# VectorE's order in the last layer's slots: the residue of the MLP tile ahead of the product for the heads

## The reference, cut to what matters

```python
# _L3_cond_ref: a dense MLP and the two best of 8 expert MLPs, hidden width 1024 each
g = einsum('bsh,hi->bsi', x, gate_w); u = einsum('bsh,hi->bsi', x, up_w)
cond = sum over (shared, top1, top2) of  w * einsum('bsi,ih->bsh', gelu(g) * u, down_w)
# _L3_ffn_ref
h = rmsnorm(cond, gamma1)
q = h @ Wq + bq                          # 16 heads of 16
k, v = split((h @ Wdown + bdown) @ Wup + bup)
att = softmax(einsum('bthd,btgd->bthg', q, k) / 4)   # per token, head against head
x1 = cond + (einsum('bthg,btgd->bthd', att, v) @ Wo + bo)
gate = softmax(rmsnorm(x1, gamma2) @ Wg + bg)
out = x1 + einsum('btd,edf,bte->btf', rmsnorm(x1, gamma2), We, gate)     # 8 experts
```

## Time and profile before

| | |
|---|---|
| median of 3 runs | 1732.6 us (1729.36 to 1734.81) |
| profiled execution, own time | 1735.44 us |
| its span | 1733.7 us |
| PE busy (matmul) | 1502.1 us, 87% |
| DVE busy | 1148.6 us, 66% |
| POOL busy | 652.6 us, 38% |
| ACT busy | 560.7 us, 32% |
| mean granted clock of PE | 0.917 of full |

### The profile page before, as it was taken

One profiled execution on the slowest core, in us unless ns is written; L12 is line 12 of the kernel. 1 busy time (PEld: TensorE's weight loads), 2 busy tenths in 40 slices (PEclk: granted clock), 3 DMA queues, 4 the chain that ended last, 5 costly groups with the idle time before them and its releaser, 6 DMA issues.

```text
span 1733.7 us, 19836 instructions
## 1 busy us (share of the span) xinstructions
PE 1502.1 (87%) x7420; PEld 1271.0 (73%) x7420; DVE 1148.6 (66%) x1977; ACT 560.7 (32%) x786; POOL 652.6 (38%) x268
## 2 busy tenths in 40 slices
PE   5997899999889978999998898987899889976628
PEld 4896799997668967899976676766677667755416
DVE  7597655546875976544568523378748975896984
ACT  2202243442232022344323343533452345332001
POOL 3320133322322201333222344366656654754552
PEclk9897989998998979899989899999999999996758
DMA  5300011111112100111111132221221212100001
GB/s 178 111 25 13 25 37 50 49 38 37 37 55 67 36 1 25 49 42 46 37 37 45 55 115 76 89 70 58 74 79 53 93 55 80 67 25 25 25 16 45
DMA packets 22592, 92.72 MB, mean 53 GB/s; under 512 B 3408, under 2 KB 3808, under 8 KB 22368
## 3 DMA queue, kind: packets, MB, share of 16 engines
q1 hardware_dynamic: 21168, 88.18, 15.4%
q10 hardware_dynamic: 1328, 3.27, 0.5%
HBM read 89.35 MB, written 2.10 MB: 53 GB/s over the span
## 4 chain that ended last, share of the span: by engine, by line
PE 34%; DVE 17%; POOL 7%; issue 7%; ACT 4%; DVEq 0%; POOLq 0%; ACTq 0%
PE bank L291 11%; PE bank L295 10%; PE bank L294 10%; POOL w_lo L413 4%; DVE G L313 3%; ACT w_hi L1030 2%; DVE bank L1532 2%; POOL VW L313 2%; DVE acc L1556 2%; DVE F L1556 1%; PE bank L759 1%; DVE acc L1688 1%; DVE hid_hi L1485 1%; PE bank L558 0%; PE bank L574 0%
## 5 line engine op out<-in xcount | busy, mean ns | idle before, releaser
L413 POOL TENSOR_TENSOR w_lo<-raw,w_hi 128x1536 fp32r<-128x1536 f32 x48 | 169.3, 3526 | 291.3 <-ACT w_hi L1030 265.6
L291 PE MATMUL bank<-x_hi,w_hi 128*128 128x512 f32 x448 | 188.3, 420 | 63.0 <-POOL w_lo L413 38.3
L401 POOL CAST w_hi<-raw 128x1024 fp32r<-128x1024 f32 (+2 forms) x42 | 49.8, 1185 | 481.4 <-issue 447.1
L1409 DVE TENSOR_TENSOR hid_lo<-F,hid_hi 128x1024 fp32r<-128x1024 f32 x64 | 82.3, 1288 | 166.6 <-ACT hid_hi L980 166.4
L294 PE MATMUL bank<-x_lo,w_hi 128*128 128x512 f32 x448 | 182.2, 407 | 0.0
L295 PE MATMUL bank<-x_hi,w_lo 128*128 128x512 f32 x448 | 181.6, 405 | 0.0
L291 PEld LDWEIGHTS bank<-x_hi,w_hi 128*128 128x128 f32 x448 | 89.2, 199 | 93.8 <-POOL w_lo L413 48.8
L404 POOL TENSOR_TENSOR w_lo<-raw,w_hi 128x1024 fp32r<-128x1024 f32 (+2 forms) x51 | 129.2, 2534 | 65.6 <-ACT w_hi L903 62.2
L975 ACT ACTIVATE F<-bank,vecs 128x512 f32<-128x512 f32 x128 | 81.2, 686 | 199.3 <-PE bank L295 199.3
L291 PE MATMUL bank<-hid_hi,w_hi 128*128 128x512 f32 x320 | 127.9, 400 | 11.4 <-DVE hid_lo L1487 6.5
L294 PE MATMUL bank<-hid_lo,w_hi 128*128 128x512 f32 x320 | 126.1, 394 | 0.0
(11 more groups left out here) (331 smaller groups left out, 4072.0 us busy)
## 6 DMA issues: line engine op xcount, KB each, us to landing
raw<-in_skill SPq DMA_DIRECT2D x32, 768.0 KB, 4.2
raw<-in_l SPq DMA_DIRECT2D x40, 512.0 KB, 3.5
raw<-in_shared SPq DMA_DIRECT2D x16, 768.0 KB, 4.2
K<-in_l3e SPq DMA_DIRECT2D x16, 512.0 KB, 3.6
raw<-in_l0c SPq DMA_DIRECT2D x12, 512.0 KB, 3.6
raw<-in_qkv SPq DMA_DIRECT2D x8, 768.0 KB, 4.2
xT<-in_x ACTq DMA_DIRECT2D x4, 512.0 KB, 7.1
VW<-in_l1w SPq DMA_DIRECT2D x1, 2048.0 KB, 8.9
```

Source lines behind the costliest of these rows:

```text
L291: i = nc.tensor.matmul(out, sh, mh, start=first, stop=False)
L413: nc.gpsimd.tensor_tensor(w_lo[n % W3_SLOTS][:], raw[n % 2][:], w_hi[n % W3_SLOTS][:].bitcast(F32), ALU.subtract).then_inc(w_ready.sem, 1)
L1409: v.tensor_tensor(hid_lo[u][:, hs, :], F[u][:], hid_hi[u][:, hs, :].bitcast(F32), ALU.subtract).then_inc(e1_hid.sem, 1)
```

## The change

In `hidden_lo`'s place: VectorE's queue gets the residue of the hidden tile right behind the gated product (and behind the special steps of that slot), and the product of the attention behind it. Nothing else moves, on VectorE or elsewhere.

```diff
                         finish3_first(p, i, x, y)
                     if 0 <= q < BATCH:
                         attention3_first(q, i, x, y)
+                    if b < BATCH:
+                        hidden_lo(TILES3 * b + i)
                     for h in range(16):
                         if HALF_SLOT[h] == i and 0 <= q < BATCH:
                             product(q, h)
                         if HALF_SLOT[h] == i + TILES3 and 0 <= p < BATCH:
                             product(p, h)
-                    if b < BATCH:
-                        hidden_lo(TILES3 * b + i)
```

## The result

The changed kernel takes 1753.2 us (median of 4 runs, 1749.96 to 1757.23) where the kernel before takes 1733.7 (4 runs). The ratio is 1.0119, 95% interval 1.0099 to 1.0138: 1.2% slower, some 20 us. The forecast was 1751.1.

What follows compares the result with a forecast made beforehand. VectorE's queue was taken to set the slots' length. Terms 8.3 + 2.6 - 1.6 + 9.2 = 18.5 us on a median of 1732.6 gave 1751.1 us; the range was 1738 to 1761, the forecast's own 1744 to 1756 (0.60).

Steps and rivals of the forecast that it cites:

- VectorE's queue sets the slot: Product slots: the gated product mostly starts when VectorE's last sum ends, so VectorE's queue sets a slot's length.
- The wait, 0.66 to 1.41: After the gated product VectorE stands from 0.66 to 1.41 us, 0.75 us, for ScalarE's high part before the residue.
- A plain pair at 12.16: Even and odd slot without other steps: odd product waits for GpSimd's sweep, 12.16 us for 10.91; 7 pairs, +8.3 us.
- Rival 2, the plain wait: Each bound slot pays 0.75, products last as before, a pair gives back 0.58: 14.2 us in all, 1747; chance 0.13.
- Slots 20 and 21, +0.2 and twice +1.2: Pairs of slots 20 and 21: +0.2 in pass 1, +1.2 each in passes 2 and 3, sum +2.6 us.
- w_lo held by 0.2: Plain pair: GpSimd's w_lo, due at 2.94 us, is held by the even product to 3.15.
- Expert slots 7.3, 7.3, 8.2, 7.3, 8.2: Slots 13 to 17, passes 2 and 3: these lengths, 38.3 us for 33.61, +4.6 a pass, +9.2 in all.
- Slots 10 to 12 cost nothing: Passes 2 and 3: slot 10's wait for PE and the gate's small steps in 11 and 12 cover the wait; 0.
- Slot pairs with another step, -1.6: Passes 2 and 3: slots 2 and 3 give -0.6 each, slots 22 and 23 -0.5 and +0.1; sum -1.6 us.
- PE gains nothing: Last layer's down matmuls: PE gets the residue earlier, gain between nothing and -3.1 us, taken as 0.
- Rival 3, the clock: PE idles longer; lower clock for half of a pair adds 0.9 in each of some 10 pairs, 1760; chance 0.12.

Runs made afterwards that it cites:

- odd and even alone: Kernel before with the residue ahead of the product in odd slots only, or in even slots only: odd 1.0058, 1744.6 us; even 1.0062, 1743.0 us.
- the tiny sweeps: GpSimd's products cut to 16 of 1024 columns, in the kernel before (1711.5 us, 0.9875) and in the changed one (1730.7 us, 0.9990).
- The exchange of the sums: Changed kernel with the sum of GpSimd's product ahead of the sum of VectorE's own: 1761.6 us, 1.0156 to the kernel before.

## Why the prediction was right, point by point

- *VectorE's queue sets the slot.* Right; odd and even alone, the tiny sweeps and the changed kernel all show slots that are the sum of VectorE's steps.
- *The wait, 0.66 to 1.41.* Right: 1.40 to 1.42 after the gated product in the plain pairs, with 0.66 to 0.67 of idle, and 1.35 in slots 0 and 1 of passes 2 and 3; 38 more residues wait for ScalarE than before, as worked out.
- *A plain pair at 12.16.* 12.21, and by the mechanism that was worked out; shown by the two halves of the change and by the tiny sweeps. The pair of slots 10 and 11 took 12.33. Rival 2, the plain wait, had the odd products as long as before (1.76); it is out.
- *Slots 20 and 21, +0.2 and twice +1.2.* Passes 2 and 3 gave +1.4 each. Pass 1 gave -0.7, which no term forecast: that is PE's clock, and luck for the sum.
- *w_lo held by 0.2.* Right, 0.15.
- *Expert slots 7.3, 7.3, 8.2, 7.3, 8.2.* 7.36, 7.36, 8.28, 7.35, 8.24. The step from them to the sum has a slip: 38.3 less 33.61 is 4.7 and not 4.6, so the term should have been +9.4.
- *Slots 10 to 12 cost nothing.* The term was a little too low, +0.1 in slots 11 and 12 each.
- *Slot pairs with another step, -1.6.* Only -0.6. Slots 2 and 3 gave -0.35 each: w_lo, held by slot 2's product, lets the sweep start 0.15 later, and the sum's 0.11 below does the rest. Slots 22 and 23 gave -0.4 and +0.5. In slots 3 and 23 alone the order pays.
- *PE gains nothing.* Right, 3.1 to 3.6 us.
- Rival 3, the clock: the mean granted clock went from 0.917 to 0.914; in the four plain pairs of slots 10 to 17 of pass 1 it was 0.93, before 0.96. So it fell a little, but no gated product in a plain pair waited for PE except that of slot 11 in pass 1, 0.26 us, where it had waited 1.15. The rival's price of 0.9 a pair didn't come.

The sum was 2.4 us low, the net of terms that came out 3.3 higher and 0.9 lower (slots 20 and 21 of pass 1). One thing was missed that runs through many of the terms: the sum of VectorE's own product took its place right behind the product, and has to wait for its write. It starts 1.25 us after the product, where the residue used to start 1.14 after. So the residue had covered two things, ScalarE's 0.75 (under the product) and this 0.11. I took steps' distances from rows in which the neighbour was independent. The exchange of the sums shows the term alone: 5.41 for 5.53. It accounts for the +0.5 of slots 10 to 12 and, with the slip of 0.2, more than covers the +0.8 of the expert slots. It isn't the whole: the later sweep in slots 2 and 3, the long product in slot 11 of pass 1 and slots 22 and 23 of pass 3 are the others.

What stays open: the runs of one kernel scatter from 1724.2 to 1736.9 over 18 (median 1733.3), and the two profiles differ by 3.4 us in layers where both execute the same instructions. Which stretch of those layers it is, wasn't looked into. In the last layer one source can be named. Slot 10 of passes 2 and 3 waits for PE, is not touched by the change in its length, and takes 10.85 us in one profile and 12.48 in the next: the same 62 matmuls, at a granted clock of 0.84 in the kernel before and of 0.73 with odd slots only. Slot 4 has such a step too: 8.66 us at 0.80 in pass 3 with the tiny sweeps and the changed order, 7.12 at 1.00 with the old one. That is 1.5 of the gap of those two profiles. Between the kernel before and the changed one these slots agree within 0.1 us, so they don't touch the result; why the clock falls in one profile and not in the next stays open.

## What to carry to other kernels

Before an instruction that waits for another engine is moved up in a queue, see what stands between it and its producer: if that filler is the queue's only cover and the queue has no slack, the move turns it into idle time, and the earlier result must have a waiter to be worth it. Where instructions of VectorE with two inputs in SBUF stand beside GpSimd's, work out a slot from who issues first, not from the sum of the times: a shift of 0.7 us can make an operation twice as long. The small ones count as well: two steps of under 0.2 us became 5.4 us when GpSimd's work was moved onto them. And the same move can pay in the few slots where the filler is itself held up.

## What the runs showed of the hardware that was not expected

- A product of VectorE that is held goes, from the release on, 1.04 to 1.08 us to an independent successor, and 1.14 when it isn't held. Where both engines had one queued, they took turns in every case seen (w_lo, product, sweep).
- A product issued 0.08 us behind an instruction of GpSimd was held for all of its 2.4 us, and one of 128x4 elements that takes 0.16 us alone lasted 3.14 behind w_lo. Sums over a product (one input in SBUF), at 1.20 to 1.22 us, and the residue (one input in PSUM), at 0.67 to 0.69, were never longer beside any instruction of GpSimd in these profiles.
- A wait for the write of the instruction just ahead costs VectorE 0.11 to 0.12 us over an independent successor (1.25 us after the product for 1.13; 5.53 us a slot for 5.41).
